# A Mamba-style mixer on one NeuronCore: the slot's order rewritten, two multiplications moved to ScalarE, and the sum of squares folded

## What is computed

```python
proj = x @ in_proj_w.T                      # gate, hBC, dt
hBC = silu(conv1d(hBC) + conv_b)            # 4 taps, causal, per channel -> hs, B, C
dt = clip(softplus(dt + dt_bias)); xch = hs * dt
L = exp(segsum(dt * A))                     # within a chunk of 128 tokens
Y_diag = (C B^T * L) @ xch                  # inside the chunk
states = carried from chunk to chunk, decayed, plus B^T (decay * xch)
Y = Y_diag + C @ state * exp(A_cum) + hs * D
g = Y * silu(gate)                          # 8 groups of 1024 channels
out = g * rsqrt(mean(g*g over the group) + eps) * norm_w
x = x + out @ out_proj_w.T
```

## Time and profile before

| What | Value |
|---|---|
| Median of 3 runs | 2931.42 us (2930.26 to 2935.69) |
| The profiled execution | 2935.76 us, span 2934.0 us |
| Mean granted clock of TensorE | 0.958 |
| PE busy | 2590.2 us, 88% of the span |
| DVE busy | 2150.2 us, 73% |
| ACT busy | 1275.0 us, 43% |
| POOL busy | 621.1 us, 21% |

### The profile page before, as it was taken

The page is one execution under the profiler, slowest core; times in us unless marked ns, Lnnn a source line. Parts: engine busy times, 40 slices in busy tenths (PEclk is TensorE's granted clock), DMA queues, the critical chain, the costliest instruction groups (busy, mean ns, idle before and its releaser), DMA issues. The chain is left out here.

```text
span 2934.0 us, 40765 instructions
## 1 busy us (share of the span) xinstructions
PE 2590.2 (88%) x14016; PEld 1766.8 (60%) x14016; DVE 2150.2 (73%) x3375; ACT 1275.0 (43%) x2537; POOL 621.1 (21%) x520
## 2 busy tenths in 40 slices
PE   3579989989999898998999899899698889999899
PEld 2456666666666666666666667665485444444388
DVE  5478888888788878878878888887554646777364
ACT  2344545454453544544445444543222236666421
POOL 2122222212213222221321312223211011110031
PEclk7789999999999999999999999999798889999999
DMA  2322222223222222221322222211102401111000
GB/s 105 78 56 62 61 75 66 54 55 86 56 68 71 64 57 78 66 53 53 87 59 63 75 59 63 79 45 30 76 0 83 165 28 39 39 39 33 1 11 18
DMA packets 194992, 172.58 MB, mean 59 GB/s; under 512 B 31264, under 2 KB 157296, under 8 KB 193136
## 3 DMA queue, kind: packets, MB, share of 16 engines
q1 hardware_dynamic: 189344, 168.13, 20.5%
q10 hardware_dynamic: 5456, 2.00, 0.3%
HBM read 151.70 MB, written 18.38 MB: 58 GB/s over the span
## 5 line engine op out<-in xcount | busy, mean ns | idle before, releaser
L490 PE MATMUL bank<-xh,wh 128*128 128x512 f32 x1152 | 478.9, 416 | 110.7 <-DVE G L824 61.4
L624 PE MATMUL bank<-wo,yt 128*128 128x512 f32 x1024 | 468.1, 611 | 3.8 <-DVE yt L879 2.1
L490 PE MATMUL bank<-xh,wl 128*128 128x512 f32 x1152 | 458.7, 398 | 0.0
L490 PE MATMUL bank<-xl,wh 128*128 128x512 f32 x1152 | 456.5, 396 | 0.0
L790 DVE SCALAR_TENSOR_TENSOR cacc<-raw,cwh,cacc 128x512 f32<-128x512 f32 x480 | 398.7, 831 | 11.3
L624 PEld LDWEIGHTS bank<-wo,yt 128*128 128x128 f32 x1024 | 200.2, 198 | 232.4 <-issue 229.0
L490 PEld LDWEIGHTS bank<-xh,wh 128*128 128x128 f32 x1152 | 220.1, 191 | 165.2 <-DVE G L824 70.1
L698 ACT COPY xs<-bank 128x512 f32<-128x512 f32 x128 | 75.1, 587 | 449.9 <-PE bank L516 449.9
L674 ACT ACTIVATE cth<-cacc 128x512 f32<-128x512 f32 x160 | 102.2, 639 | 346.7 <-DVE cacc L790 346.5
L490 PEld LDWEIGHTS bank<-xh,wl 128*128 128x128 f32 x1152 | 220.3, 191 | 50.3
L490 PEld LDWEIGHTS bank<-xl,wh 128*128 128x128 f32 x1152 | 221.1, 192 | 40.3
(11 more groups left out here) (248 smaller groups left out, 4951.4 us busy)
## 6 DMA issues: line engine op xcount, KB each, us to landing
xn<-w_hs_dram SPq DMA_DIRECT2D x112, 256.0 KB, 2.7
EC<-ecum_scratch SPq DMA_DIRECT2D x112, 256.0 KB, 8.3
xn<-w_gate_dram SPq DMA_DIRECT2D x80, 256.0 KB, 3.0
wo<-w_out_dram SPq DMA_DIRECT2D x8, 2048.0 KB, 8.2
rawx<-w_gate_dram SPq DMA_DIRECT2D x48, 256.0 KB, 3.0
rawx<-w_hs_dram SPq DMA_DIRECT2D x48, 256.0 KB, 2.7
qk_scratch<-at_part SPq DMA_DIRECT2D x48, 256.0 KB
at_qT<-qk_scratch SPq DMA_DIRECT2D x32, 192.0 KB, 2.6
```

What stands on the lines that cost most here:

```text
L490: mm = nc.tensor.matmul(BA[bank][:, :], w[:, s, k, :], x[:, k, tok], start=(k == 0 and m == 0), stop=(k == KC - 1 and m == 2))
L624: mm = nc.tensor.matmul(BA[b][:, :], yt[:, j * P:(j + 1) * P], wo[:, j, :], start=(j == 0), stop=(j == JT - 1))
```

## The change

Five things are done in the mixer; the other layers are as before.

1. dt times hs is done by ACT while it copies the transposes out of PSUM: 16 activations of 128x64, one per head, with dt as scale from a column of `pk`, in place of two copies of 128x512 to `xs` and one DVE product of 128x1024.
2. The output weights are multiplied by `norm_w` by ACT, in 8 activations of 128x512 in four pairs between its other work of slot z=0, in place of one POOL instruction of 128x4096. `wo_set` rises after the last pair.
3. The squares lie in a tensor of their own, `sq`. DVE adds the upper half to the lower half twice (512, then 256 elements), and PE sums the two blocks left with two matmuls, ahead of the last conv tile; in slots without conv tiles after the output product.
4. The order in the slot: PE does `pe_pre`, `pe_hidden` 0 and `pe_diff` 0, 1 of nxt ahead of `ydiag`, and the state product and `pe_diff` 2, 3 after both gate tiles. ACT has relu 0, 1 between the two gate tanhs. DVE does `dv_small` right after yoff's decay, both gate tiles before the state, and the masking in three pieces. Each conv tile's taps come before the low part of the weights.
5. SP asks for `RW` two slots ahead, after the slot's two gate loads; `EC` is first.

The skip product `hd` stays on POOL, as do `xd`, the state's decay and the power.

```diff
         def pe_slot(pe, g, z, tiles, bank, last):
...
+        def pe_squares(pe, g, z, last):
+            n = 8 * g + z
+            dv_sq.wait(pe, 2 * n + 2)
+            if not last:
+                ac_xc.wait(pe, 2 * n + 3)
+            for j in range(2):
+                mm = nc.tensor.matmul(BT[1][:, 0:1], sq[:, j, :], ones1[:, :], start=(j == 0), stop=(j == 1))
+            mm.then_inc(pe_ss.sem, 1)
...
+            if not last:
+                pe_pre(pe, *nxt)
+                pe_hidden(pe, *nxt, 0)
+                pe_diff(pe, *nxt, (0, 1))
+
+            ac_xc.wait(pe, 2 * n + 2)
...
+            if not last and mine:
+                pe_hidden(pe, *nxt, 1)
+            if step:
+                for u in range(2):
+                    release_a(pe, g, z, u)
+                    pe_tile(pe, step, "gate", 2 * (z % CH) + u, bank())
+            if z < NT - 1:
                 po_xd.wait(pe, skip_last(g, z, 1) + 1)
...
+            if not last:
+                pe_diff(pe, *nxt, (2, 3))
+                if not mine:
                     pe_hidden(pe, *nxt, 1)
...
+            for r in range(len(mine)):
+                if r == len(mine) - 1:
+                    pe_squares(pe, g, z, last)
+                tile(r)
             pe.wait_ge(wo_set, 17 * g + 17)
...
-            dv_sq.wait(pe, n + 1)
-            if not last:
-                ac_xs.wait(pe, 2 * n + 3)
-            nc.tensor.matmul(BT[1][:, 0:1], sqs[:, :], ones1[:, :], start=True, stop=True).then_inc(pe_ss.sem, 1)
+            if not mine:
+                pe_squares(pe, g, z, last)
...
+        def ac_xdt(act, g, z, u):
...
+            for i in range(HG // 2):
+                hh = u * (HG // 2) + i
+                o = nc.scalar.activation(xch[:, hh * HP:(hh + 1) * HP], BT[1 - u][:, i * HP:(i + 1) * HP], ACT.Copy,
+                                         scale=pk[:, h, c, O_DT + hh:O_DT + hh + 1])
+            o.then_inc(ac_xc.sem, 1)
+
+        def ac_weigh(act, g, i):
+            act.wait_ge(wo_set, 17 * g + 16)
+            act.wait_ge(d_pk[0], 48 * g + 48)
+            for j in (2 * i, 2 * i + 1):
+                o = nc.scalar.activation(wo[:, j, :], wo[:, j, :], ACT.Copy, scale=nw[:, 0, j:j + 1])
+            if i == JT // 2 - 1:
+                o.then_inc(wo_set, 1)
...
             if not last:
-                ac_exps(act, *nxt, (0, 1))
+                ac_xdt(act, *nxt, 0)
+                if mine:
+                    ac_xdt(act, *nxt, 1)
+            if step:
+                ac_gate_tanh(act, step, 2 * (z % CH), bank())
+            for p, i in left:
+                ac_tile_tanh(act, p, i)
+            if not last:
+                ac_relu(act, *nxt, 0)
+                ac_relu(act, *nxt, 1)
+            if step:
+                ac_gate_tanh(act, step, 2 * (z % CH) + 1, bank())
+            if not last:
+                ac_exp(act, *nxt, 0)
+                ac_exp(act, *nxt, 1)
+            dv_gg.wait(act, n + 1)
+            pe_ss.wait(act, n)
+            nc.scalar.activation(sq[:, :, :], yt[:, :].rearrange("p (j t) -> p j t", j=JT), ACT.Square).then_inc(ac_sq.sem, 1)
+            if not last:
+                ac_relu(act, *nxt, 2)
+                ac_relu(act, *nxt, 3)
             copy(0)
...
+            weigh(0)
             if not last:
...
+                ac_exp(act, *nxt, 2)
+                ac_exp(act, *nxt, 3)
+                if not mine:
+                    ac_xdt(act, *nxt, 1)
+            copy(1)
+            tanh(0)
+            weigh(1)
             copy(2)
             tanh(1)
...
+            weigh(2)
             copy(3)
+            weigh(3)
             tanh(2)
...
+        def dv_fold(dve, n, i):
+            m = JT >> (i + 1)
...
+            nc.vector.tensor_tensor(sq[:, 0:m, :], sq[:, 0:m, :], sq[:, m:2 * m, :], ALU.add).then_inc(dv_sq.sem, 1)
...
+            if not last:
+                dv_masked(dve, *nxt, (0,))
+            dv_fold(dve, n, 0)
+            if not last:
+                dv_masked(dve, *nxt, (1,))
+            dv_fold(dve, n, 1)
...
             conv(0)
             conv(1)
             silu(0)
+            if not last:
+                dv_masked(dve, *nxt, (2, 3))
             conv(2)
             silu(1)
...
             if z == 0:
-                po_weigh(pool, g)
                 po_taps(pool, g, 1)
...
                         for u in range(2):
                             next_tile(number(step, "gate", 2 * (z % CH) + u) + WR)
+                    next_rows(8 * g + z + 2)
+                    for i in mine:
+                        next_tile(number(step, "conv", i) + WR)
```

More of the change, by code:

```diff
@@ L710, in ac_slot @@
         def ac_slot(act, g, z, tiles, bank, last):
             n = 8 * g + z
-            h = z // CH
             nxt = (g, z + 1) if z < NT - 1 else (g + 1, 0)
             step, mine = tiles
[L715 to L724, removed]
+            left = left_over(g, z)
@@ L879, in dv_slot @@
             nc.vector.tensor_tensor(yv, yv, gate_chunk(h, c), ALU.mult).then_inc(dv_gg.sem, 1)
-            if mine and not last:
-                dv_small(dve, *nxt)
-            for p, i in left_over(g, z):
+            left = left_over(g, z)
+            for p, i in left:
                 dv_conv_tile(dve, p, i)
-            if mine and not last:
-                dv_xdt(dve, *nxt)
-            for p, i in left_over(g, z):
+            if step:
+                dv_gate_tile(dve, step, 2 * (z % CH), bank(), n + 1)
@@ L901, in dv_slot @@
-            for u in range(2):
-                if step:
-                    dv_gate_tile(dve, step, 2 * (z % CH) + u, bank(), n + 1)
-                if not mine and u == 0:
-                    state()
-                    if not last:
-                        dv_small(dve, *nxt)
-            if mine:
-                state()
-            elif not last:
-                dv_xdt(dve, *nxt)
+            if step:
+                dv_gate_tile(dve, step, 2 * (z % CH) + 1, bank(), n + 1)
+            if z < NT - 1:
+                for u in range(2):
+                    cols = slice(u * 512, (u + 1) * 512)
+                    pe_st.wait(dve, skip_last(g, z, 2) + u + 1)
+                    if z > 0:
+                        po_s1.wait(dve, skip_both(g, z) + 1)
+                        nc.vector.tensor_tensor(st[:, cols], st[:, cols], BY[u][:, :], ALU.add).then_inc(dv_st.sem, 1)
+                    else:
+                        pe_yo.wait(dve, skip_first(g, 0, 2))
+                        nc.vector.tensor_copy(st[:, cols], BY[u][:, :]).then_inc(dv_st.sem, 1)
@@ L1073, in _ @@
                     next_tile(q)
+                next_rows(1)
                 def slot_loads(g, z, end):
-                    if not (end and z == NT - 1):
-                        next_rows(g, z)
+                    if z < NT - 1:
+                        next_decay(g, z)
                     if z == 0 and not end:
@@ L1082, in slot_loads @@
                     if step:
-                        for kind, i in [("gate", 2 * (z % CH)), ("gate", 2 * (z % CH) + 1)] + [("conv", i) for i in mine]:
-                            next_tile(number(step, kind, i) + WR)
+                        for u in range(2):
+                            next_tile(number(step, "gate", 2 * (z % CH) + u) + WR)
+                    next_rows(8 * g + z + 2)
+                    for i in mine:
+                        next_tile(number(step, "conv", i) + WR)
                     if end:
```

174 lines of the change are left out of this document (57 added, 117 removed).

## The result

The changed kernel takes **2804.0 us** (median of 4 runs, 2803.16 to 2806.64) against 2933.56 us (4 runs, 2930.26 to 2935.73): ratio 0.9561, 95% interval 0.9544 to 0.9577, or 4.4% faster. Its profiled execution took 2806.64 us (span 2804.8), 129.1 less than the one of before. The experiments ran on other chips, so they are compared by their ratios to before; 0.001 of ratio is 2.9 us.

A forecast was written before the change was run, and what follows sets the result against it. TensorE, 92% busy in the mixer, bounds the kernel. From 2935.8 us: less 142.0 waits, 6.2 prologue, 32 clock; plus 15.4 squares, 9 z=7, 42.8 and 11.7 z=0, 1.3 prologue: 2836 us, own range 2813 to 2869, stated range 2780 to 2900.

The forecast's parts named there:

- The likeliest case: Whole kernel: the forecast itself, 2836 us with own range 2813 to 2869, given a 55% chance.
- The order, 142.0 us of waits: Mixer slots: TensorE's waits for gate tile (60.0), sum of squares (37.0), `dv_small` (30.4) and relu (14.6) all go.
- Squares, +15.4 us: Every mixer slot: two matmuls with ones instead of one, 0.24 us more in each of 64 slots.
- first rival: Slots with three conv tiles: folds come late after meeting `xd`, about 2 us in 30 slots, 60 us, 2896; 22%.
- dt on ScalarE: ScalarE's 16 small activations: 0.24 us each, 3.8 a slot, hidden by TensorE's tile except 1.3 us in the prologue.
- second rival: ScalarE's small activations cost 0.67 each like large ones; second differences wait 3.3 us in 45 slots, 147 us, 2983; 8%.
- Output weights, +42.8 us: Slot z=0: TensorE's output product waits 5.3 us for the fourth weight pair, eight times.
- clock behind it: Slot z=0, behind the output-weights wait: slower TensorE clock costs 1.46 us each time, 11.7 in all.
- third rival: Slot z=0: ScalarE runs further ahead, no wait for output weights; 42.8 and 11.7 come back, 2782 us; 12%.
- z=7, +9 us: Slot z=7, without state product: second differences wait for the relus, 1.3 us in 7 slots.
- The prologue, -6.2 and +1.3 us: Prologue: `ydiag` no longer meets the product on `wo`, 6.2 gained; ScalarE's small activations are not hidden, 1.3 lost.
- `RW`, taken at nothing: New DMA order: `RW`'s later request costs nothing; 40 us if its landing took 12 us.

The follow-up runs named there:

- e9: Changed kernel keeping only the new order: dt product back on VectorE, reduce and one matmul for the folds, output weights on GpSimd; 2845.6 us, ratio 0.9682.
- e12: e5 with the reduce and one matmul in place of the two folds and two matmuls; 2719.3 us, ratio 0.9255.
- e5: e2 and e4 together on the changed kernel, with the last weight pair weighed ahead of the last conv tile's copies; 2733.2 us, ratio 0.9308.
- e2: Changed kernel, but z=0's output product waits for each pair of weight blocks, not for all four pairs ahead of the first; 2741.6 us, ratio 0.9335.
- e11: e2 and e3 together on the changed kernel: weights waited for pair by pair, reduce in place of the folds; 2749.2 us, ratio 0.9359.
- e7: Changed kernel with the product by dt in 64 activations of 128x16 in place of 16 of 128x64; 3185.9 us, ratio 1.0854.
- e3: Changed kernel with one reduce and one matmul in place of the two folds and two matmuls, place in the order kept; 2803.9 us, ratio 0.9547.
- e4: Changed kernel with the squares' matmuls behind the output product in every slot, folds left where they are; 2794.6 us, ratio 0.9515.
- e8: Changed kernel with ScalarE's dt activations undone: two copies of 128x512, VectorE multiplies by dt in place; 2827.9 us, ratio 0.9634.
- e6: Changed kernel with the product by dt in 32 activations of 128x32 in place of 16 of 128x64; 2826.2 us, ratio 0.9627.

## Why the prediction was right, and where its sum was off

The likeliest case came true: the waits of the earlier trace rows went, and the one forecast for z=0 came, at the length forecast. The time is 32 us (1.1%) below the forecast, 29 when both are taken from the profiled executions, and that is 9 us under the forecast's own range of 2813 to 2869. Errors of the sum stand on both sides, so the closeness owes something to luck. Step by step:

- **The order, 142.0 us of waits.** Right: they are gone, and e9 shows that the order does most of it. The walk through the slot had the second fold at 19.0 and TensorE's want of it at 19.1. In the slot that starts at 1120.31 the fold ends at 18.77, and TensorE, by its pitch, wants it at 18.66: the places are right to 0.5 us, and which of the two comes first is not.
- **Squares, +15.4 us.** Right in size: the second matmul costs 0.24 a slot, by e12 against e5. The first rival (a fold or the low part meets `xd`) happened in small: `wl` took 1.75 us behind `xd`, the fold came just too late, and the squares cost 0.3 us more in 23 slots. That is 7 us (e5 against e2), which the forecast put at nothing and the rival at 60. The Trainium skill (SBUF — State Buffer, "Who interferes with whom") has two inputs in SBUF contend with GpSimd's reads, and these rows agree. Its other half, that the reduce doesn't contend, no run here tests: the reduces that meet a GpSimd product at all share at most 0.26 us with it (e11). Ahead of the last tile the 1.89 us of the old form were simply the longer ones.
- **dt on ScalarE.** Taken at 0.24 apiece, measured 0.20; nothing followed from it, as TensorE's tile hides it. By the Trainium skill (ScalarE: Activation LUTs, "What ACT_TABLE_LOAD costs") the estimates are 0.24, 0.21 and 0.20 for 64, 32 and 16 columns; measured 0.20, 0.17 and 0.156 are all lower. The second rival was priced by its waits alone; e7 shows that the clock adds about half as much again.
- **Output weights, +42.8 us.** Right: 5.67 a group for the 5.35 forecast. The **clock behind it was mis-sized**: 3.06 a group, not 1.46, so +24.5 for +11.7. I had taken the loss behind a wait of 2.84 us for one of 5.3. Undoing the wait gave back 65 us (e2), so the wait cost some 10 us more than the 54.5 that the third rival had allowed for it.
- **z=7, +9 us.** Wrong: no wait. I took 9.9 us for the left-over conv from a slot in which `hd` delays it. In z=7 `hd` needs that tile's own silu, as it prepares the next group, so it starts only behind it; the conv takes 2.32 us where the next z=1 takes 3.96, and the relus are in time (VectorE's timeline after):

```profile
1069.69 2.32 DVE L813 SCALAR_TENSOR_TENSOR cacc<-raw,cwh,cacc 128x512 f32<-128x512 f32 x3
...
1127.28 3.96 DVE L813 SCALAR_TENSOR_TENSOR cacc<-raw,cwh,cacc 128x512 f32<-128x512 f32 x3
```

- **The prologue, -6.2 and +1.3 us.** The 6.2 are gone; the longest wait for a relu, 1.9, stands there. `RW`, taken at nothing, is waited for once, 0.7 us, there too.
- **Missing: `yoff`.** Its 2.05 us held a wait that no list shows, and that was taken for a price: `ydiag`, right behind it, waits for the first half of VectorE's decay product and starts 0.10 us after that half's end in 55 of 56 slots. With `pe_pre` between them `yoff` takes 1.78. Of the 0.27 us, 0.18 is the wait. The other 0.09 goes with the squares' matmul, which stood right ahead of `yoff`: where it stands there again, with `pe_pre` behind, `yoff` takes 1.86 (e12). Together they make about 14 us. The last slot of all has no `pe_pre`, and there `yoff` still takes 2.04 in the changed kernel:

```profile
1922.58 2.03 PE L551 MATMUL bank<-act,st 128*128 128x128 f32 x16
1924.62 1.97 PE L570 MATMUL bank<-em,xch 128*64 128x128 f32 x32
```
- **Waits and clock in the other slots.** A wait costs TensorE more than its row. In the slot at 1007 us before, the row for `dv_small` says 1.74, but the distance between starts is 1.89 over its pitch; 0.15 in each of the 116 waits of the earlier trace rows is, by this estimate, 17 us. The output product of that slot took 8.22 (1023.97 to 1032.19) for 6.87. With its second differences, some 1.8 us of clock were lost there rather than 1.46: about 5 us more.

From 100 less: 9 for z=7, 14 for `yoff`, 17 and 5 for the last point; the other way 15 for z=0 (2.5 of wait, 12.8 of clock) and 7 for the squares. That is 123 of 129 us; nothing run here divides the other 6. The waits' excess is read from a single slot and was not run by itself.

## What to carry to other kernels

A wait that replaces another is to be priced with the clock behind it, and removed before parts are compared: e2, one wait cut into four, gained 66 us, and e3, e4 and e8 each got 5 to 9 us back behind it that had nothing to do with their edit. Reordering alone brought 93 of the 129 us, and a lighter engine only what its slack was worth at the points where it had come just too late; such points are found by putting the end of the producer beside the time at which the consumer, by its own pitch, would start. A start just behind the producer's end is a wait, also where no list shows one. A pitch taken from the old trace can hold a wait of its own when the instruction behind it depends on another engine.

## What the runs showed of the hardware

- What the clock costs behind a wait is not fixed by the wait's length. In the changed kernel the eight output products behind the waits of 5.67 us took 9.93 to 9.98 us each, 3.1 over their pitch; behind eight waits of 5.74 they took between 8.53 and 10.01 in e4, and from 9.91 down to 8.42 in e3. The granted clock was 0.70 over the 9.93 us behind the wait in the changed kernel, and 0.84 over 9.55 in the group of e3 that is shown. The Trainium skill (TensorE: Matmul & The Clock Gate, "Part 1: The HAM clock gate") says that the number of slow matmuls varies from run to run of one kernel; here it varies from one wait to the next in one execution, and no run shows why.
- A matmul of 128x1 in float32 takes 0.14 us from its start to the next one's when nothing is waited for (e12), 0.24 just behind a wait; two take 0.36 (e4) and, behind a wait, 0.47.
- Small activations have a fixed part: 0.156, 0.170 and 0.20 us for 16, 32 and 64 columns (e7, e6 and the changed kernel).
